# A decoder layer in split fp32: the gated layers' rows of batches 2 to 7 transposed by TensorE, and the checks of the weight sums put into other waits

## The reference, cut to what matters

```python
x = x + attn(layernorm(x), w_q, w_k, w_v, w_o)                  # 16 heads of 64, causal
x = x + xattn(layernorm(x), ctx, ctx, mask, Wq, bq, Wk, bk, Wv, bv)  # 64 keys per batch
n = layernorm(x)
h = silu((n @ w1.T) * s1) * ((n @ w2.T) * s2)                   # the gated layer
h = gelu((h @ h1.T) * sh1)
h = gelu((h @ h2.T) * sh2)
x = x + (h @ w3.T) * s3
```

## Time and profile before

| what | value |
|---|---|
| three timed runs, median (lowest to highest) | 1486.34 us (1485.69 to 1489.36) |
| the profiled execution's own time | 1484.85 us |
| its span, first to last instruction | 1483.1 us |
| busy: TensorE, VectorE, ScalarE, GpSimd | 98%, 85%, 69%, 33% of the span |
| the gated and first hidden layers of batches 1 to 6 | about 868 to 1166 us, a batch each 49.9 us |

### The profile page before, as it was taken

One profiled execution on the slowest core, in us unless ns is written; L12 is line 12 of the kernel. 1 busy time (PEld: TensorE's weight loads), 2 busy tenths in 40 slices (PEclk: granted clock), 3 DMA queues, 4 the chain that ended last, 5 costly groups with the idle time before them and its releaser, 6 DMA issues.

```text
span 1483.1 us, 29119 instructions
## 1 busy us (share of the span) xinstructions
PE 1451.1 (98%) x10408; PEld 1221.6 (82%) x10408; DVE 1256.1 (85%) x3072; ACT 1020.3 (69%) x2382; POOL 483.4 (33%) x755
## 2 busy tenths in 40 slices
PE   8999999999999999999998999999999999999998
PEld 6888888888888888888887787877786888888887
DVE  8999999999999999999999777779777847888876
ACT  6888888888888888887888853564455445655544
POOL 2545655546545555555444021102112100000000
PEclk9999999999999999999999999999999999999999
DMA  4000100001001010010012543543442493041310
GB/s 157 2 1 2 58 2 32 28 2 59 1 16 44 1 58 2 2 58 2 22 65 72 190 150 139 200 145 119 142 158 99 156 344 126 30 143 59 115 57 31
DMA packets 78277, 114.59 MB, mean 77 GB/s; under 512 B 4768, under 2 KB 54304, under 8 KB 77216
## 3 DMA queue, kind: packets, MB, share of 16 engines
q1 hardware_dynamic: 78112, 112.37, 22.2%
HBM read 72.50 MB, written 42.99 MB: 78 GB/s over the span
## 4 chain that ended last, share of the span: by engine, by line
PE 77%; DVE 11%; issue 7%; ACT 2%; POOL 2%; DMA 1%; SPq 0%; DVEq 0%; POOLq 0%
PE bank L1362 11%; PE bank L757 10%; PE bank L677 9%; PE bank L729 8%; PE bank L679 8%; PE bank L678 8%; PE bank L741 6%; PE bank L1206 4%; PE bank L1208 4%; PE bank L1380 4%; PE bank L1321 1%; PE bank L1323 1%; PE bank L1332 1%; PE bank L1325 1%; DVE PT L827 1%
## 5 line engine op out<-in xcount | busy, mean ns | idle before, releaser
L948 POOL TENSOR_SCALAR P<-P,stats 128x512 f32<-128x512 f32 (+3 forms) x512 | 268.1, 545 | 329.8 <-DVE stats L926 329.7
L813 ACT ACTIVATE P<-P,stats 128x384 f32<-128x384 f32 (+3 forms) x512 | 284.1, 561 | 17.4 <-DVE stats L918 17.2
L780 ACT ACTIVATE PT<-bank 128x512 fp32r<-128x512 f32 (+1 forms) x384 | 185.4, 525 | 86.4 <-PE bank L741 85.4
L918 DVE CUSTOM_DVE_ANT_0 P<-bank,cmask 128x384 f32<-128x384 f32 (+3 forms) x512 | 228.4, 483 | 1.2 <-PE bank L729 0.9
L827 DVE TENSOR_TENSOR PT<-bank,PT 128x512 fp32r<-128x512 f32 (+1 forms) x384 | 218.4, 594 | 4.9 <-ACT PT L780 4.2
L1362 PE MATMUL bank<-op,ws 128*128 128x512 f32 x896 | 205.9, 389 | 0.0
L1206 PE MATMUL bank<-Hb,hw 128*128 128x512 f32 x512 | 202.0, 395 | 1.3 <-DVE Hb L1565 1.2
L1362 PEld LDWEIGHTS bank<-op,ws 128*128 128x128 f32 x896 | 167.3, 188 | 34.2
L757 PEld LDWEIGHTS bank<-PT,V 128*128 128x128 f32 x1024 | 164.8, 190 | 23.0 <-DVE PT L827 4.3
L757 PE MATMUL bank<-PT,V 128*128 128x512 f32 (+3 forms) x1024 | 175.9, 319 | 3.5 <-DVE PT L827 3.5
L1208 PE MATMUL bank<-Hb,hw 128*128 128x512 f32 x448 | 174.8, 390 | 0.0
(11 more groups left out here) (240 smaller groups left out, 3150.5 us busy)
## 6 DMA issues: line engine op xcount, KB each, us to landing
h_scratch<-go SPq DMA_DIRECT2D x64, 256.0 KB, 2.1
src<-h_scratch SPq DMA_DIRECT2D x16, 1024.0 KB, 6.6
xs<-x_scratch SPq DMA_DIRECT2D x15, 512.0 KB, 4.0
ws<-ws_scratch SPq DMA_DIRECT2D x7, 1024.0 KB, 7.5
stageA<-in_h SPq DMA_DIRECT2D x10, 512.0 KB, 4.4
x_scratch<-x SPq DMA_DIRECT2D x8, 512.0 KB, 3.2
x_scratch<-xs SPq DMA_DIRECT2D x8, 512.0 KB, 3.7
stageC<-in_h SPq DMA_DIRECT2D x16, 256.0 KB, 4.2
```

The lines of the kernel that those rows point to most:

```text
L780: return e.activation(dst, src, ACT.Copy, scale=scale)
L813: e.activation(p, p, ACT.Exp, bias=st_[:, k:k + 1], scale=-1.0, accum_out=st_[:, 8 + k:9 + k]).then_inc(s_exp, 1)
L918: e.tensor_tensor_reduce(P_tile(P, i, a), banks["S", P, max(i, 1)][a][:, slice(*S_COLS[i])], cmask[:, 512 - n:512], -1.0, 3.0e38, ALU.add, ...
L948: e.tensor_scalar(p, p, stats[P % 4][:, k:k + 1], 1.0, ALU.mult, ALU.mult).then_inc(s_norm, 1)
```

## The change

`tv` is gone. `by_pe(b, which)` is true for the gated layer's rows of every batch and for the scores' rows of batches 0 and 1; where it is true, `xt` on TensorE transposes, and `xth` and `xtl` read its banks. So for batches 2 to 7 the two `xt` steps stand behind `h` 6 of the batch before, where the halves already stood.

`sumlook` of a sum moves from behind `h` 6 into the softmax of a later batch, between `xs4` and `xr`, and the next sum's loads and adds (`sumld`, `sums`) follow it there. `sumst` moves from behind `h` 5 to behind `h` 3. The last sum has a tile of its own (`stageD`, at the place of `xtt`); sums 6 and 7 are checked in batch 7, behind `h` 0 and `h` 1. The `look`s are eight in place of ten: four blocks of `h2` are looked at by halves of 512 columns, two halves in one load tile. Flag 1 and its transpose move back by one `h` in batch 7.

```diff
+def by_pe(b, which):
+    return which == 1 or b < BY_BLOCK
@@ def later():
     def xs(b):
-        return [(f"xs{k}", b) for k in range(1, 5)] + [("xe", b), ("xr", b)]
+        o = [(f"xs{k}", b) for k in range(1, 5)] + [("xe", b)]
+        if b > 1:
+            o.append(("sumlook", b - 2))
+        if b:
+            o += [("sumld", b - 1), ("sums", b - 1)]
+        return o + [("xr", b)]
     def xt(b, which):
-        return [(k, b, which, j) for k in ("xt", "xth", "xtl")[b >= BY_BLOCK:] for j in range(2)]
+        return [(k, b, which, j) for k in ("xt", "xth", "xtl")[not by_pe(b, which):] for j in range(2)]
     def norm(b, which):
-        return [(k, b, which) for k in ln] + [("tv" if which else "tt", b)] * (b >= BY_BLOCK)
+        return [(k, b, which) for k in ln] + [("tt", b)] * (not by_pe(b, which))
...
-            if 0 < b < 6 and m < 2:
+            if 0 < b < 5 and m < 2:
                 o.append(("look", 2 * b - 2 + m))
-            if (0 < b < 6 and m == 0) or (b < 5 and m == 2):
+            if (0 < b < 5 and m == 0) or (b < 4 and m == 2):
                 o.append(("lookld", look))
                 look += 1
-            if b < 6 and m in SUM_AT:
-                o.append((SUM_AT[m], b))
-            if b == 6 and m in LAST_SUMS:
-                o.append(LAST_SUMS[m])
+            if b < B - 1 and m == (4 if b == 0 else 3):
+                o.append(("sumst", b))
+            if b == B - 2 and m in (3, 5):
+                o += [("sumld", 7), ("sums", 7)] if m == 3 else [("sumst", 7)]
+            if b == B - 1 and m < 2:
+                o.append(("sumlook", 6 + m))
             if b == B - 1:
-                o += [("flag", 1)] * (m == 0) + [("ft", 1), ("fm", 1)] * (m == 2)
+                o += [("flag", 1)] * (m == 1) + [("ft", 1), ("fm", 1)] * (m == 3)
@@
+    stD = at(L + 88, "stageD", [128, 1024])
@@ lnorm, on VectorE
-                w.wait_ge(s_x2T, min(2 * LN.index((b, which)), 4 * BY_BLOCK))
-                if which and b >= BY_BLOCK:
-                    w.wait_ge(s_xtt, 4 * (b - BY_BLOCK + 1))
-                elif b > BY_BLOCK:
-                    w.wait_ge(s_xtv, b - BY_BLOCK)
+                n = LN.index((b, which))
+                if n:
+                    last = LN[n - 1]
+                    if by_pe(*last):
+                        w.wait_ge(s_x2T, xt_by_pe[last + (1,)])
+                    else:
+                        w.wait_ge(s_xtt, 4 * (last[0] - BY_BLOCK + 1))
@@ on VectorE
-            elif kind == "tv":
-                b = a[0]
-                w.wait_ge(s_ln2, ln_at(b, 1) + 4)
-                w.wait_ge(s_x2lo, xt_at(b, 0))
-                for r in range(4):
-                    for q in range(4):
-                        rs, qs = slice(32 * r, 32 * r + 32), slice(32 * q, 32 * q + 32)
-                        x = xns[rs, :, :].rearrange("p t (k q j) -> p q k t j", k=2, q=4)[:, q]
-                        y = xtd[qs, :].rearrange("p (k t r i) -> p r k t i", k=2, t=NT, r=4)[:, r]
-                        i = e.transpose(y, x)
-                i.then_inc(s_xtv, 1)
@@ sumld, on SP's queue
-                w.wait_ge(s_slook, j)
+                if j == 7:
+                    w.wait_ge(s_xts, 16 * (B - BY_BLOCK))
+                else:
+                    w.wait_ge(s_slook, j)
```

More of the change, by code:

```diff
@@ L211 @@
 BY_BLOCK = 2
-SUM_AT = {2: "sumld", 3: "sums", 5: "sumst", 6: "sumlook"}
-LAST_SUMS = {0: ("sums", 6), 1: ("sumst", 6), 2: ("sumlook", 6), 3: ("sumld", 7), 4: ("sums", 7), 5: ("sumst", 7), 6: ("sumlook", 7)}
+def by_pe(b, which):
+    return which == 1 or b < BY_BLOCK
 def later():
@@ L278, in later @@
                     o.append(("sumcp", b - 1))
-                if (b, m) == (6, 5):
-                    o.append(("sumld", 6))
                 if b == B - 1 and m == 5:
@@ L1028, in program @@
     s_x2T, s_x2hi, s_x2lo = sem("s_x2T"), sem("s_x2hi"), sem("s_x2lo")
-    s_xtt, s_xtv, s_xts, s_xtd = sem("s_xtt"), sem("s_xtv"), sem("s_xts"), sem("s_xtd")
+    s_xtt, s_xts, s_xtd = sem("s_xtt"), sem("s_xts"), sem("s_xtd")
     s_xk, s_xkf, s_xkhi, s_xklo = sem("s_xk"), sem("s_xkf"), sem("s_xkhi"), sem("s_xklo")
@@ L1101, in program @@
     stage3 = [stA[:, :], xsf]
-    looks = [A["h2"][m] for m in range(8)] + [A["w3"][:, 0:1024], A["w3"][:, 1024:2048]]
+    looks = [[A["h2"][m]] for m in range(4)]
+    looks += [[A["h2"][m + i][:, 512:1024] for i in range(2)] for m in (4, 6)]
+    looks += [[A["w3"][:, 0:1024]], [A["w3"][:, 1024:2048]]]
     SET = (0, 1, 2, 4, 6, 5, 3)
@@ L1142, in slot_free, with sum_stage @@
         return (s_go, n) if q % 2 == 0 else (s_out, 2 * n)
+    def sum_stage(j):
+        return stD if j == 7 else stC
     def ln_at(b, which):
@@ L1151, in xt_rows @@
     def xt_rows(b, which, j):
-        if b < BY_BLOCK:
+        if by_pe(b, which):
             return bank["xt", b, which, j][:, :]
-        if which:
-            return xtd[:, 512 * j:512 * j + 512]
         return xtd[:, :].rearrange("p (a k t i) -> p k a t i", a=4, k=2, t=NT)[:, j]
@@ L1161, in xt_parts @@
         x = XTs[:, k, j, :]
-        return x if b < BY_BLOCK or which else x.rearrange("p (t a i) -> p a t i", t=NT, a=4)
+        return x if by_pe(b, which) else x.rearrange("p (t a i) -> p a t i", t=NT, a=4)
+    xt_by_pe = counted("PE", "xt")
     def xt_at(b, which):
@@ L1423, in act_rest @@
                 b, which, j = a
[L1424 to L1427, removed]
+                if by_pe(b, which):
+                    w.wait_ge(s_x2T, xt_by_pe[b, which, j])
                 else:
@@ L1760, in dve_rest @@
                 bits = stA[:, :].bitcast(i32)
-                w.wait_ge(s_look, 16 * (k + 1))
+                w.wait_ge(s_look, 16 * (k + 1 + max(0, k - 3) - max(0, k - 5)))
                 e.tensor_scalar(bits, bits, 0xFFF, None, ALU.bitwise_and).then_inc(s_and, 1)
@@ L1770, in dve_rest @@
                 j = a[0]
-                bits = stC[:, :].bitcast(i32)
-                w.wait_ge(s_sst, 16 * j + 16)
+                bits = sum_stage(j)[:, :].bitcast(i32)
+                w.wait_ge(s_sst, 16 * (8 if j > 5 else j + 1))
                 e.tensor_scalar(bits, bits, 0xFFF, None, ALU.bitwise_and).then_inc(s_sand, 1)
@@ L1835, in dve_rest @@
                         w.wait_ge(s_w3lo, 2)
-                        w.wait_ge(s_xtv, B - BY_BLOCK)
+                        w.wait_ge(s_x2T, len(xt_by_pe))
                 else:
@@ L1873, in pool_rest @@
                 j = a[0]
-                x = [stC[:, 256 * q:256 * q + 256] for q in range(4)]
+                x = [sum_stage(j)[:, 256 * q:256 * q + 256] for q in range(4)]
                 w.wait_ge(s_sld, 32 * j + 32)
@@ L1948, in sp_rest @@
                 w.wait_ge(s_rest, k)
-                e.dma_start(stA[:, :], looks[k]).then_inc(s_look, 16)
+                n = 1024 // len(looks[k])
+                for i, part in enumerate(looks[k]):
+                    e.dma_start(stA[:, i * n:i * n + n], part).then_inc(s_look, 16)
             elif kind == "w3":
@@ L1963, in sp_rest @@
                         w.wait_ge(*s)
-                w.wait_ge(s_slook, j)
+                if j == 7:
+                    w.wait_ge(s_xts, 16 * (B - BY_BLOCK))
+                else:
+                    w.wait_ge(s_slook, j)
                 for i in range(2):
-                    e.dma_start(stC[:, 512 * i:512 * i + 512].rearrange("p (h f) -> p h f", h=2),
+                    e.dma_start(sum_stage(j)[:, 512 * i:512 * i + 512].rearrange("p (h f) -> p h f", h=2),
                                 A["h2"][m + 4 * i].rearrange("p (h f) -> p h f", h=2)[:, :, cs]).then_inc(s_sld, 16)
@@ L1978, in sp_rest @@
                 e.dma_start(ws_d[2:6, :, cs].rearrange("s p f -> p s f"),
-                            stC[:, :].rearrange("p (s f) -> p s f", s=4)).then_inc(s_sst, 16)
+                            sum_stage(j)[:, :].rearrange("p (s f) -> p s f", s=4)).then_inc(s_sst, 16)
             elif kind == "wld":
```

## The result

The changed kernel takes 1472.24 us (median of four runs, 1471.96 to 1474.60), the kernel before 1486.01 us (four runs): a ratio of 0.9906, 95% interval 0.9888 to 0.9924. The forecast was 1473.0 us. It was faster, by 13.8 us where 13.3 us were worked out.

A forecast was written before the change was run, and what follows sets the result against it. TensorE, busy 98% of the span, was taken to bound the kernel. Its waits of 18.6 us would go for 5.3 us of added transposes: 13.3 us gained from 1486.34, so 1473.0 us, range 1470 to 1479.

The forecast's parts named there:

- (a): TensorE's loss between `h` 7 and `u` 0: 1.99 us in batches 2 to 6, 1.02 in batch 7, sum 10.9 us.
- (b): TensorE's loss around the start of `u` 4, waiting for `hm` 0: 0.90 us in batches 2 to 6, sum 4.5 us.
- (c): Loss at the end of `h` 0, last `hl` late: 0.25 us in four batches, 2.2 in batch 6, sum 3.2 us.
- The price of the transposes: Eight added on TensorE behind `h` 6 of six batches: 0.89 us a batch, 5.3 us in all.
- its large case: End of `h` 0 in batch 6: 2.2 us lost, with weight sum 6 on GpSimd beside the last `hl`.
- The moved steps: Sums, checks, loads and stores at new places: check hidden behind the exponentials with 1.1 us left, queues and banks cost nothing.
- fifth `u` waits: Rival: `u` 4 still waits for VectorE's chain to `hm` 0; gain 8.8 us, time 1477.5 us; chance 0.10.
- Transposes overlap: Rival denied this: transposes cost their whole duration on TensorE, 13.1 to 15.8 us, time 1483 us; chance 0.05.
- The late rows: Rival: TensorE waits for normalized rows ahead of `h` 7; slower, 1491 us at 3 us more lateness; chance 0.05.

## Why the prediction was right

*The losses (a), (b), (c).* All three went, as the sum had it: 18.6 us of loss for 5.3 us of transposes, 13.3 against 13.8 measured. ((a) adds up to 11.0 and not 10.9, which changes nothing.) Within the traces the distance from `g` 0 of batch 1 to `g` 0 of batch 7 fell by 13.4 us (six periods of 47.44 against 298.1).

*The price of the transposes* was the term with the widest bounds, 0.89 to 2.2 us a batch. Batch 1 was the right row: 0.88 us measured, and 0.87 for eight more.

*What makes (a).* Here the result was right and the reason only half of it. I put (a) down to the 16 blocks, and booked the norm of 3.19 us, slowed by the sum beside it, only as more time to spare. It was 1.8 of the 2 us: taking the sum away removes (a) with the blocks in place. Batch 1, which I called the best evidence for (a), could not tell the two apart: it has the transposes on TensorE, but its sum also ends before its norm begins, so that norm takes 1.39 us. These are the last addition and the norm of batch 1 in the trace of before:

```profile
856.65 0.74 POOL L1881 TENSOR_TENSOR stageC<-stageC 128x256 f32<-128x256 f32 x1
```

```profile
861.31 1.39 DVE L1625 TENSOR_SCALAR xns<-xs,sm 128x256 f32<-128x256 f32 x4 [1.14 <-POOL sm L1857]
```

That the transposes remove (a) as well, even beside a slow norm, was therefore not in evidence; the run with the transposes alone shows it. So the sum of the change is not "transposes gain 10.9 and cost 5.3": the moved sums alone would have gained it, and the moved transposes alone as well. Once both are made, the transposes only cost, but for the 0.2 us a batch that the sums alone leave. The prediction did not see that the transposes are the part to leave out: the kernel with the sums alone takes 1467.84 us, 4.2 us less than the changed one, the fastest of all.

*What makes (b)* was right: the check and the late chain ahead of `hm` 0. Moving the check alone removed it in the four batches where it was moved; the transposes alone removed it too, with the check left in its place.

*(c), its large case.* Right in kind: the sum 6 beside the last halves. With the transposes alone 1.25 us of it stay, where 2.2 were lost; that this is because VectorE is no longer late there is argued, not tested.

*The moved steps.* Check hidden with 1.1 us left (1.21 measured), queues and banks without a wait, as worked out.

*The rivals.* No fifth `u` waits. Transposes overlap. The late rows did not come about: 4.9 us to spare where 4.8 were forecast, and the sum ended 2.9 us before the power was wanted. Their price was too low, though: I had each microsecond cost one; the run that forces a wait of 2.35 us shows 2.5, and 1.6 more wherever the clock falls.

What stays open: the runs do not tell why the clock fell after three of six equal waits, and a difference of some 1 us between a median and the sum of its trace, as with the doubled transposes, is not explained. The executions of the doubled transposes have a mean granted clock of 0.997 to 0.999, those of the changed kernel beside them 0.998 to 0.999, which goes the same way.

## What to carry to other kernels

Where a chain is late by 2 us, ask of every instruction in it whether it runs at its own speed: the same norm took 1.4 us alone and 3.2 beside GpSimd's sums, and one wait that kept them apart was worth 10 us. When two edits aim at the same wait, price each alone, for the second finds nothing left to gain and may still cost.

## What the runs showed of the hardware

A wait of TensorE may cost more than its length: after three of six waits of 2.35 us the granted clock fell to 0.60 over 4.3 us, and each took 1.5 to 1.6 us more. Between 870 and 1170 us the kernel before, with waits of up to 1.5 us, and the changed kernel, with none, have a granted clock of 1.00. Outside the changed part the kernel before shows the same fall: TensorE stands 2.93 us for `PT` until 802.65, and the mean granted clock over the 4.3 us from there is 0.63 (a row of the timeline, then a stretch, as above).

```profile
802.65 4.10 PE L757 MATMUL bank<-PT,V 128*128 128x512 f32 x16 [2.93 <-DVE PT L827]
```

```profile
802.60:806.90 4.30, 4.25 (x18) 3.97 (x19) 4.20 (x14) 1.55 (x4) 1.37 (x1) 0.63 0.33 122
```

A VectorE instruction may be slowed by GpSimd and hardly slow it in turn: the norm took 3.19 us beside the additions and 1.38 us without them, the additions 3.10 and 3.07 us. Beside the subtractions of batch 6 both took longer.
